# A cross-attention block: half of the probabilities turned by transposing DMAs in place of TensorE

## The reference

```python
q = split_heads(layernorm(x) @ Wq + bq)            # 16 heads of 32, 128 queries
k = split_heads(ctx @ Wk + bk)                     # 2048 keys
v = split_heads(ctx @ Wv + bv)
attn = softmax(einsum('bhqd,bhkd->bhqk', q, k) / sqrt(32))
out = einsum('bhqk,bhkd->bhqd', attn, v)           # then @ Wo + bo, added to x
```

## Time and profile before

| | |
|---|---|
| median of 3 runs | 515.18 us (515.12 to 515.43) |
| profiled execution, its own time | 515.1 us |
| its span in the trace | 513.3 us |
| TensorE, VectorE, ScalarE, GpSimd busy | 96%, 60%, 52%, 8% of the span |
| granted TensorE clock, mean | 0.998 of full speed |

### The profile page before, as it was taken

The page is one execution under the profiler, slowest core; times in us unless marked ns, Lnnn a source line. Parts: engine busy times, 40 slices in busy tenths (PEclk is TensorE's granted clock), DMA queues, the critical chain, the costliest instruction groups (busy, mean ns, idle before and its releaser), DMA issues.

```text
span 513.3 us, 9255 instructions
## 1 busy us (share of the span) xinstructions
PE 495.2 (96%) x3742; PEld 378.2 (74%) x3742; DVE 307.7 (60%) x585; ACT 266.2 (52%) x401; POOL 42.2 (8%) x34
## 2 busy tenths in 40 slices
PE   8999998999999999999999999999899998999995
PEld 6786777777777777897877778757595866877663
DVE  3757532645554553346187384579379978975962
ACT  4230037495857641328357748467345727755730
POOL 0030000000199000000000000000002010000000
PEclk9999999999999999999999999999999999999999
DMA  8900000000341022220310000298387899876001
GB/s 277 357 2 1 1 1 0 2 1 1 108 162 64 1 77 89 82 83 1 106 39 3 0 3 0 68 421 334 109 324 271 316 390 377 298 298 240 1 0 41
DMA packets 11497, 63.52 MB, mean 124 GB/s; under 512 B 1600, under 2 KB 2112, under 8 KB 4544
## 3 DMA queue, kind: packets, MB, share of 16 engines
q1 hardware_dynamic: 11168, 62.67, 32.3%
q10 hardware_dynamic: 288, 0.27, 0.2%
HBM read 62.41 MB, written 0.52 MB: 123 GB/s over the span
## 4 chain that ended last, share of the span: by engine, by line
PE 83%; ACT 7%; DVE 5%; issue 4%; POOL 0%; POOLq 0%; ACTq 0%; DVEq 0%
PE ps L1155 36%; PE ps L1225 11%; PE ps L1239 6%; PE ps L1209 5%; ACT Pm L452 4%; PE ps L1471 3%; PE ps L1473 3%; PE ps L1472 3%; PE ps L1491 3%; PE ps L1430 1%; PE ps L1431 1%; PE ps L1432 1%; PE ps L1149 1%; PE ps L1420 1%; ACT PT L460 1%
## 5 line engine op out<-in xcount | busy, mean ns | idle before, releaser
L753 DVE TENSOR_SCALAR_CACHE_REDUCE Pm<-ps,small 128x512 f32<-128x512 f32 x96 | 66.4, 748 | 30.5 <-PE ps L1209 30.3
L460 ACT COPY PT<-ps 128x512 f32<-128x512 f32 x128 | 68.5, 592 | 28.9 <-PE ps L1225 28.9
L1225 PE MATMUL ps<-ident,Pm 128*128 128x128 f32 x512 | 69.3, 277 | 3.2 <-ACT Pm L452 3.2
L1225 PEld LDWEIGHTS ps<-ident,Pm 128*128 128x128 f32 x512 | 56.5, 141 | 18.0 <-issue 11.0
L452 ACT ACTIVATE Pm<-Pm,small 128x2048 f32<-128x2048 f32 x32 | 64.3, 2011 | 3.5 <-DVE Pm L753 3.5
L733 DVE SCALAR_TENSOR_TENSOR KrL<-ps,small,KrH 128x512 fp32r<-128x512 f32 x32 | 23.9, 747 | 61.2 <-ACT KrH L438 61.2
L1155 PE MATMUL ps<-wvH,ctxH 128*128 128x512 f32 x124 | 50.3, 405 | 1.0 <-DVE V L742 1.0
L1155 PE MATMUL ps<-ctxH,wkH 128*128 128x512 f32 x124 | 51.1, 412 | 0.0
L1155 PE MATMUL ps<-ctxL,wkH 128*128 128x512 f32 x124 | 48.6, 392 | 0.0
L1155 PE MATMUL ps<-ctxH,wkL 128*128 128x512 f32 x124 | 48.5, 391 | 0.0
L1155 PE MATMUL ps<-wvH,ctxL 128*128 128x512 f32 x124 | 48.4, 390 | 0.0
(11 more groups left out here) (229 smaller groups left out, 872.3 us busy)
## 6 DMA issues: line engine op xcount, KB each, us to landing
w1raw<-in_W SPq DMA_DIRECT2D x16, 1024.0 KB, 6.1
w2raw<-in_W SPq DMA_DIRECT2D x16, 1024.0 KB, 7.3
raw<-in_ctxT SPq DMA_DIRECT2D x7, 1024.0 KB, 5.2
woF<-in_ffn_Wo SPq DMA_DIRECT2D x4, 1024.0 KB, 10.0
wo<-in_wo SPq DMA_DIRECT2D x2, 1024.0 KB, 4.9
ctx_first<-in_ctxT SPq DMA_DIRECT2D x4, 256.0 KB, 4.7
wv_raw<-in_xWv SPq DMA_DIRECT2D x2, 512.0 KB, 8.2
wq<-in_xWq SPq DMA_DIRECT2D x1, 1024.0 KB, 13.3
```

Source lines behind the costliest of these rows:

```text
L460: act.copy(PT[:, c % 2, i, :, :].rearrange("p k t -> p (k t)"), ps[:, t_bank(p, c, i), :]).then_inc(pt_done, 1)
L753: dve.tensor_scalar(Pm[:, i, c * CH:(c + 1) * CH], ps[:, i, :], -1.0, mx[:, p % 2, i, c - 1:c] if c else NOT_YET, ALU.mult, ALU.min, accum ...
L1225: last = pe.transpose(ps[:, t_bank(p, c, i), j * P:(j + 1) * P], Pm[:, i, c * CH + j * P:c * CH + (j + 1) * P], ident[:])
```

## The change

In steps 0 to 6 only chunks 0 and 1 (`PEC = 2`) are turned on TensorE. Chunks 2 and 3 take another way. For each head, GpSimd takes the 1024 float32 words apart into their upper and lower 16-bit halves, in two copies, into one of two staging buffers (`stage`, which lies over slot 1 of `PT`). SP issues one transposing DMA for each head, which writes the 2048 half-words, turned in 16 blocks of 128x128, back over the same part of `Pm`. When all four heads are there, GpSimd joins the halves in `PT`, two copies for each head and chunk. Step 7 is turned on TensorE as before.

What moves with it: chunks 0, 1 and 3 share slot 0 of `PT` (`slot_user` says which product a write waits for), chunk 2 has slot 1. `negative_scores` of chunks 2 and 3 waits for the merges. TensorE's order in a pass is written anew: transposes of chunks 0 and 1 as before, then scores 1, keys 3, product 1, scores 2, product 2, scores 3. The split of entry 1's context goes from GpSimd to ScalarE (the casts, in pass 3) and VectorE (the subtractions of chunks 1 to 3), with the subtraction of chunk 0 left on GpSimd between splits and merges. The `rsqrt` calls stand among the splits and merges. SP's context loads stand between transposing DMAs.

```diff
+        def by_dma(p, c):
+            return p < NP - 1 and c >= PEC
...
+        def pt_slot(p, c):
+            return c % 2 if p == NP - 1 else int(c == PEC)
+
+        def slot_user(p, c):
+            if p == NP - 1:
+                return C * p - 1 if c == 1 else C * p + max(c - 1, 0)
+            return {0: C * p, 1: C * p + 1, 2: C * p - 1, 3: C * p + 2}[c]
...
+            def turned(p, i):
+
+                sp.wait_ge(p_split, 2 * (HPG * p + i + 1))
+                sp.dma_start_transpose(Pm[:, i, PEC * CH:].bitcast(U16).rearrange("p (k t) -> p k t", t=T),
+                                       stage[:, i % 2, :, :, :].rearrange("p c h n -> p (c h n)")).then_inc(p_turned[i % 2], 16)
...
+            for p in range(G):
+                for i in range(HPG):
+                    if p == G - 2 and i != 2:
+                        context_in((0, 1, None, 2)[i])
+                    turned(p, i)
+                if p == G - 2:
+                    context_in(3)
...
+            def probs_split(p, i):
+
+                pool.wait_ge(exp_done, HPG * p + i + 1)
+                if p == G:
+                    pool.wait_ge(pv2_mm, 1)
+                if p:
+                    pool.wait_ge(pv_mm, C * (p - 1) + PEC + 1)
+                if i >= 2:
+                    pool.wait_ge(p_turned[i % 2], 16 * (2 * p + 1))
+                words = Pm[:, i, PEC * CH:].bitcast(U16).rearrange("p (c n h) -> p c n h", c=C - PEC, h=2)
+                for h in range(2):
+                    pool.tensor_copy(stage[:, i % 2, :, h, :], words[:, :, :, 1 - h]).then_inc(p_split, 1)
+
+            def probs_merged(p, c):
+
+                for k in range(2):
+                    pool.wait_ge(p_turned[k], 16 * 2 * (p + 1))
+                if slot_user(p, c) > 0:
+                    pool.wait_ge(pv_mm, slot_user(p, c))
+                for i in range(HPG):
+                    words = halves_of(PT[:, pt_slot(p, c), i, :, :].rearrange("p k t -> p (k t)"))
+                    halves = Pm[:, i, c * CH:(c + 1) * CH].bitcast(U16)
+                    for h in range(2):
+                        pool.tensor_copy(words[:, :, 1 - h], halves[:, h * CH:(h + 1) * CH]).then_inc(merged, 1)
...
+                if p == G - 1:
+                    context_high(0)
+                    context_high(1)
...
-                    if p:
-                        dve.wait_ge(t_mm, n - C * HPG + 1)
+                    if p and c < PEC:
+                        dve.wait_ge(t_mm, turned_before(p - 1, c, i) + 1)
+                    elif p:
+                        dve.wait_ge(merged, merged_before(p - 1, c, i + 1))
...
+                if p == G:
+                    context_low(2)
                 if p < NP:
                     keys(p, 2)
+                if p == G:
+                    context_low(3)
                 for c in range(C):
+                    if p == G - 1 and c == C - 1:
+                        context_low(1)
...
+                    probs_T(p - 1, 0, 0)
+                    probs_T(p - 1, 0, 1)
+                    keys(p, 2)
+                    probs_T(p - 1, 0, 2)
+                    probs_T(p - 1, 0, 3)
+                    scores(p, 0)
+                    probs_T(p - 1, 1, 0)
+                    probs_T(p - 1, 1, 1)
+                    weighted_values(p - 1, 0)
+                    probs_T(p - 1, 1, 2)
+                    probs_T(p - 1, 1, 3)
+                    scores(p, 1)
+                    keys(p, 3)
+                    weighted_values(p - 1, 1)
+                    if p == G + 3:
                         masks(0)
+                    scores(p, 2)
+                    weighted_values(p - 1, 2)
+                    scores(p, 3)
```

More of the change, by code:

```diff
@@ L238, in perceiver_block @@
         s_mm, s_done = sem("s_mm"), sem("s_done")
+        p_split, merged, ctx_first1 = (sem(n) for n in ("p_split", "merged", "ctx_first1"))
+        p_turned = [sem(f"p_turned{k}") for k in range(2)]
         exp_done, t_mm = sem("exp_done"), sem("t_mm")
@@ L312, in ffn_wo_in @@
                 sp.dma_start(woF[:, k, :], a["ffn_Wo"][:, k, :]).then_inc(woF_in, 16)
+            for p in range(G, NP - 1):
+                for i in range(HPG):
+                    turned(p, i)
             sp.wait_ge(k_mm, NP * C)
@@ L567, in while_values, with context_high @@
                 values(1, n // JT, n % JT)
+            def context_high(c):
+                act.wait_ge(raw_in[c], 32 if c else 16)
+                act.copy(ctxH[c][:], raw[c][:]).then_inc(ctx_hi1, 1)
             for p in range(1, NP + 1):
@@ L595, in _ @@
                             keys(p, 3)
-                        probs_T(p - 1, c, i)
+                        if not by_dma(p - 1, c):
+                            probs_T(p - 1, c, i)
                         if c == 3 and i == 1:
@@ L600, in _ @@
                         outputs2_T(0)
+                    if p == G - 1 and c >= 2:
+                        context_high(c)
                 if p == G:
@@ L1160, in keys @@
                 b, g = divmod(p, G)
-                if b:
-                    pe.wait_ge(ctx_split1, c + 1)
+                if b and c == 0:
+                    pe.wait_ge(ctx_first1, 1)
+                elif b:
+                    pe.wait_ge(ctx_split1, c)
                 else:
@@ L1229, in weighted_values @@
             def weighted_values(p, c):
-                n = p * C + c
-                pe.wait_ge(pt_done, HPG * (n + 1))
+                if by_dma(p, c):
+                    pe.wait_ge(merged, merged_before(p, c, HPG))
+                else:
+                    pe.wait_ge(pt_done, turned_before(p, c, HPG))
                 if c == 0 and p:
@@ L1239, in weighted_values @@
                         last = pe.matmul(ps[q, PV_BANK, 0:T], V[:, c * JT + j, (HPG * g + i) * DH:(HPG * g + i + 1) * DH],
-                                         PT[:, c % 2, i, j, :], start=(c == 0 and j == 0),
+                                         PT[:, pt_slot(p, c), i, j, :], start=(c == 0 and j == 0),
                                          stop=(c == C - 1 and j == JT - 1))
@@ L1516, in _ @@
                     pe.wait_ge(v_dve, p // G * 2 * C + 2 * C)
-                for c in range(C):
-                    probs_T(p - 1, c, 0)
-                    probs_T(p - 1, c, 1)
-                    if p == G + 3 and c == 2:
-                        masks(0)
-                    if c == 0 and more:
-                        keys(p, 2)
-                    if c == 0 and p == NP:
-                        first_experts(1)
-                    if c:
-                        weighted_values(p - 1, c - 1)
-                    probs_T(p - 1, c, 2)
-                    probs_T(p - 1, c, 3)
-                    if more:
-                        scores(p, c)
-                        if c == 1:
-                            keys(p, 3)
+                if not more:
+                    for c in range(C):
+                        probs_T(p - 1, c, 0)
+                        probs_T(p - 1, c, 1)
+                        if c:
+                            weighted_values(p - 1, c - 1)
+                        else:
+                            first_experts(1)
+                        probs_T(p - 1, c, 2)
+                        probs_T(p - 1, c, 3)
+                else:
+                    probs_T(p - 1, 0, 0)
[13 more added lines that the diff above has]
+                    if p == G + 3:
+                        masks(0)
+                    scores(p, 2)
+                    weighted_values(p - 1, 2)
+                    scores(p, 3)
                 if p == G:
```

72 lines of the change are left out of this document (46 added, 26 removed).

## The result

| | before | changed |
|---|---|---|
| median of 4 runs each, taken side by side | 515.3 us (515.12 to 516.45) | 531.6 us (530.27 to 535.85) |
| ratio, 95% interval | | 1.0326 (1.0263 to 1.0388) |
| profiled execution; its span | 515.1; 513.3 us | 530.66; 528.9 us |
| mean granted TensorE clock | 0.998 | 0.977 |

The account below looks back on a forecast made before the run. A loop over ScalarE, TensorE and VectorE was taken to bound the kernel, 27.63 us a pass. Pass gains and losses, context move included, totalled 0.0; DMA waits cost 4.8 us; against 515.1 this gave 520 us, range 509 to 590.

Parts of the forecast that it names:

- likeliest case: Whole kernel: 520 us, own range 512 to 525 with DMAs of 3.5 to 5.3 us; chance 0.45.
- the context's move: Passes 3 and 4: entry 1's casts on ScalarE and subtractions on VectorE delay loop work, together 7.6 us lost.
- What bounds the kernel: Ordinary pass: loop of ScalarE, TensorE and VectorE, 27.63 us; of 4.0 us transposes removed, 2.2 come off, net 1.4.
- Passes 1 and 2 at about 27.4: Sign expected in the profile after the change: length in us of passes 1 and 2.
- slow rival: Transposing DMA over 5.5 us (some 553 to 615 us; chance 0.30) or GpSimd copies at two-input rate (some 600; 0.12).
- One `PT` slot: Ordinary pass: copies of chunk 1 wait for chunk 0's product, so transposes of heads 2 and 3 start 0.75 us later.
- GpSimd's copies: Each pass: 8 splits of 1.02 us and 16 merges of 0.58 us, 17.4 us in all, which fits.
- The rival's 1.28 us: Merge time on GpSimd if 16-bit copies run at the two-input rate, split 2.4; some 600 us in all; chance 0.12.
- The transposing DMA: Four a pass on SP's queue, 5.0 us each to landing; late merges cost 1.2 us in passes 1, 2, 6, 7.
- Each waits for less than its neighbour: Pass 3: SP's four 1 MB loads stand between transposing DMAs, each said to wait for less than its neighbour.
- Passes 5 and 6: Pass 5: VectorE's extra work eats the gain, 0; pass 6: statistics hold the negations, gain 0.6 us before the DMA's cost.
- The faster rival: Passes 3 and 4's context work costs nothing (7.6 us back), DMA 4.6 us or less (4.8 back): 507.5 us; chance 0.13.

Follow-up runs that it names:

- the best version: Changed kernel with only steps 0, 1, 5, 6 by DMA, context on GpSimd, eight dummy products before each chunk 2 product in those passes: 511.12 us, ratio 0.9931.
- the filled version: Kernel before with the context's casts and subtractions moved, plus dummy TensorE products in two waits of passes 3 and 4: 526.51 us, ratio 1.0227.

## Why the prediction was right, and where not

The forecast, slower, holds; 531.6 lies in the range of 509 to 590, but above the likeliest case's own 512 to 525. The mechanisms it named were found, and its rivals did not decide. That the number lies in the range is in part luck: the range went up to 590 for slow DMAs and slow copies on GpSimd, and neither came. The size was 10.8 us short in the span, and nearly all of that is in two terms, the context's move and TensorE's clock.

- **What bounds the kernel: right.** A loop over three engines, in which VectorE's reading of the scores' banks takes what the transposes give: without the DMAs pass 1 gains 1.34 us of the 4.0 taken off TensorE (1.4 predicted). With the DMAs the merges take over in pass 2. The product of chunk 2 starts 23.87 us after the first exponential, in the changed kernel and in the best version (24.5 predicted), and the best version's passes gain 1.0 us (1, 2 and 7) and 0.7 (6), where 1.4 less 1.2 was 0.2. In pass 6 of the changed kernel, where the product waits 0.36 us only, VectorE's release of scores 3 is there too:

```profile
323.66 0.50 PE L1308 MATMUL ps<-KrH,qH 32*128 32x512 f32 x1 [0.18 <-DVE Pm L839]
```

- **The signs.** "Passes 1 and 2 at about 27.4" were 29.43 and 28.21. For pass 1 the figure could not come: from exponential to exponential it has 30.28 us before; 27.6 holds for stretches from keys to keys. And TensorE waits 2.08, 1.97 and 5.01 us for merges in passes 1 to 3, over the 1.5 that was to show a slow rival, though the DMAs took 4.5 us. That sign contradicted the prediction's own count, in which scores 2 end 21.5 us after the first exponential (20.6 + 0.9) and the product starts at 24.5: a wait of 3.0 in the likeliest case.
- **One `PT` slot: right**, 0.85 us for 0.75.
- **GpSimd's copies: right for the splits, low for the merges.** A split's group has 2.03 us for two, so 1.0 each (1.02 predicted). A merge takes 0.77 and they follow each other at 0.68 to 0.70 us (0.58 predicted), so a chunk's eight take 5.5 us and not 4.6. The rival's 1.28 us is excluded, but 1.2 times the estimate is where the prediction let it begin to decide.
- **The transposing DMA: right in size, low in what it costs once loads stand beside it.** 4.5 us in an ordinary pass (5.0 predicted), 5.6 as the median in pass 3. "Each waits for less than its neighbour" was wrong there: a split waited 4.32 us. All DMA time together is worth 3.3 to 4.1 us (4.8 predicted, spread over four passes). It lies in pass 3, which is 4.2 us shorter without the DMAs; the other passes are within about 1 us of the changed kernel's, up and down.
- **The context's move: right in kind, mis-sized.** This is the step that failed: "Together 7.6" measured 12.1 us. The parts alone cost 5.0 (casts) and 8.3 (subtractions), so they overlap by 1.2. The term lacked two things. TensorE's clock falls to 1.2 GHz behind waits of 2 to 5 us, so each wait is paid again in what follows it: 1.5 us in pass 3 by the keys' duration, some 3 over both passes by the estimate from the filled version. And the fourth cast ahead of an exponential costs about 0.9. The rest of the change adds 1.45 us in pass 3 and 0.6 in pass 4.
- **The clock as a term: missing altogether.** The kernel before has it at full in every slice, so no row of it has a price for its loss. Filling the waits gave back 6.9 us of 16.3, with one fall left in pass 3. The clock also accounts for the +1.5 behind pass 7 (5.24 us for 3.67), and pass 2, which loses 0.6 us, gains 0.9 with the clock held.
- **Passes 5 and 6**, +0.6 and +0.8 for 0 and +0.6: near, but for pass 6 by luck. With the clock held it is 29.99 us, 0.5 under the kernel before, so what it lost goes with the clock rather than with the DMA's 1.2.
- **The faster rival** (context work for nothing, short DMAs: 507.5) is what the best version comes near to, but by leaving passes 3 to 5 alone, not because that work found idle time.

Left open: how far the 4.2 us between the context's move alone and the whole change are merges and how far clock; passes 2 to 6 mix them, and no version of the whole change holds the clock throughout.

## What to carry to other kernels

An engine at 96% busy need not set the pace: find the loop over the engines and count only what lies on the part that the change shortens. Work that gets moved to make room for a change is priced at the instruction that stands behind it, not by the receiving engine's idle share; here it cost three quarters of the loss, and with it left where it was, and TensorE turning the probabilities in those two passes, a loss of 3.3% became one of 0.4%. Turning step 4 on TensorE too and filling the waits made it a gain of 0.7%. A new wait of TensorE can cost twice, once as the wait and once as the slower clock behind it. A few dummy products in the wait can buy the second part back; their duration is measured first (0.24 us each here, not 0.12), so that they don't outlast it.

## What the runs showed of the hardware

- **A transposing DMA from SBUF to SBUF.** 512 KB land 4.3 to 4.6 us after the issue (medians of passes 1, 2, 4, 6 and 7 of the changed kernel), 5.6 us beside the context loads of pass 3. The page counts 59840 packets under 512 bytes in the changed kernel and 1600 before; for 28 DMAs that is 2080 each, some 252 bytes a packet. While they run with nothing beside them, the fullest slices show 212 to 223 GB/s. The Trainium skill ("DMA: Bandwidth & Descriptors", Latency and other measured facts) gives 261 GB/s, measured on one kernel; this case's rows are lower, and they decide.
- **16-bit copies on GpSimd.** 1024 elements read with a stride of two take 1.04 us, 512 written with a stride of two 0.77 us. ScalarE does four of the latter in 2.67 us.
- **VectorE blocks GpSimd.** In the stretch of pass 3 in which VectorE subtracts one SBUF tile from another (163.37, 2.57 us), one of GpSimd's merges takes 2.82 us and the others 0.77 (duration ns, least, median, most):

```profile
L460 POOL COPY PT<-Pm x10: 764/770/2822, 159.7 to 167.9; 128x512 uint16<-128x512 uint16 x10
```

By the Trainium skill ("SBUF — State Buffer", Who interferes with whom) the two share a pair of ports that one holds for a whole instruction; the row agrees.
- **TensorE's clock** fell from 2.4 to 1.2 GHz behind waits of 1.97, 2.12, 3.41, 4.91 and 5.01 us, sometimes not until a few matmuls behind the wait's end (0.39 us to 179.44, 0.63 from 179.99). Behind pass 1's wait of 2.08 us it did not fall, and without the DMAs it fell behind scores that VectorE released head by head, with no wait over 0.18 us: the length of a wait alone does not tell it. Versions in which TensorE waits for merges in pass after pass spread widely from run to run (5.6 us in 4 runs of the changed kernel, 5.4 in 10 of the one with four steps by DMA); with fills the latter had 1.0 in 4 runs. The kernel before has 2.0 in 13.
